# Gathering two instead of five pairs of round one's expert results ahead of round two's last down product

## The reference, cut to what matters

```python
top_scores, top_idx = jax.lax.top_k(sigmoid(xf @ gate_w.T), 2)       # 64 experts, 2 per token
buf = zeros((64, CAP, d)).at[flat_e, pos].set(x_pairs)               # tokens sorted by expert
h = silu(einsum('ecd,edh->ech', buf, w1)) * einsum('ecd,edh->ech', buf, w3)
y = einsum('ech,ehd->ecd', h, w2)
routed = (y[flat_e, pos].reshape(-1, 2, d) * top_scores[..., None]).sum(1)
shared = silu(xf @ sw1) * (xf @ sw3) @ sw2
out = h_res + shared + routed
```

## Time and profile before

| | us |
|---|---|
| median of three timed runs | 250.8 |
| lowest and highest of them | 248.49 and 253.65 |
| span of the profiled execution, first to last instruction | 258.9 |

### The profile page before, as it was taken

How to read it: one execution, slowest core, us unless ns; L and a number is a source line. 1 busy time by engine, 2 the same in 40 slices (tenths; PEclk the granted TensorE clock), 3 DMA queues, 4 the chain that set the end, 5 groups by cost and what they waited for, 6 DMA issues and landing times.

```text
span 258.9 us, 6074 instructions
## 1 busy us (share of the span) xinstructions
PE 187.3 (72%) x2479; PEld 154.5 (60%) x2479; DVE 152.3 (59%) x366; ACT 82.7 (32%) x245; POOL 146.2 (56%) x117
## 2 busy tenths in 40 slices
PE   0067967388899796994992997589888799619810
PEld 0067856267789585892991884368667677218410
DVE  0034364956778789689579557697896173001291
ACT  2005100032343432412411342356887342023500
POOL 3336499079989599986877673101516414730270
PEclk9999999779999999797798699657999999967975
DMA  7999999999999999999999995980013292310332
GB/s 256 236 385 420 372 417 329 418 417 417 416 421 424 416 421 413 422 404 391 297 213 232 206 148 85 293 233 5 0 38 109 70 279 60 93 32 21 103 95 52
DMA packets 32981, 65.11 MB, mean 251 GB/s; under 512 B 2874, under 2 KB 25367, under 8 KB 32375
## 3 DMA queue, kind: packets, MB, share of 16 engines
q1 hardware_dynamic: 31416, 59.47, 69.7%
q10 hardware_dynamic: 576, 3.26, 3.0%
q0 software_dynamic: 960, 1.97, 2.8%
HBM read 56.96 MB, written 7.73 MB: 250 GB/s over the span
## 4 chain that ended last, share of the span: by engine, by line
PE 37%; DMA 16%; DVE 16%; SPq 8%; ACT 5%; another core or an unknown queue 5%; POOL 4%; issue 4%; POOLq 1%; DVEq 0%; ACTq 0%
DMA ring<-in_L_tok_weight_dram 15%; PE bank L840 12%; PE bank L1000 4%; SPq L360 4%; PE bank L1030 4%; DVE ring L1220 3%; DVE bank L1250 3%; POOL ring L464 2%; DVE prod L1241 2%; PE bank L1014 2%; SPq L366 2%; PE bank L974 2%; PE bank L883 1%; PE bank L903 1%
## 5 line engine op out<-in xcount | busy, mean ns | idle before, releaser
L464 POOL TENSOR_TENSOR ring<-ring,mask 128x896 f32<-128x896 f32 (+1 forms) x48 | 92.1, 1945 | 18.4 <-DMA ring<-in_L_tok_weight_dram 18.4
L840 PE MATMUL bank<-ring,xT 128*64 128x128 f32 x1248 | 85.4, 295 | 10.6 <-DVE ring L1220 6.6
L840 PEld LDWEIGHTS bank<-ring,xT 128*64 128x64 f32 x1248 | 77.1, 149 | 16.1 <-DVE ring L1220 8.1
L1220 DVE TENSOR_TENSOR ring<-ring,bank 128x1024 f32<-128x1024 f32 (+1 forms) x45 | 45.7, 1048 | 34.7 <-DMA ring<-in_L_tok_weight_dram 34.6
L453 POOL TENSOR_TENSOR rstd<-mv,half 128x1 f32<-128x1 f32 (+1 forms) x24 | 14.3, 603 | 38.3 <-DVE mv L1228 22.8
L531 POOL DMA_INDIRECT ring<-expert_outputs,slot_index x16 | 16.1, 1007 | 26.6 <-DMA expert_outputs<-ring 22.3
L1000 PE MATMUL bank<-w,ring 128*64 128x128 f32 (+1 forms) x256 | 17.0, 322 | 8.0 <-ACT ring L692 5.7
L1000 PEld LDWEIGHTS bank<-w,ring 128*64 128x64 f32 (+1 forms) x256 | 12.9, 146 | 11.4 <-ACT ring L692 6.5
L506 POOL TENSOR_TENSOR mask<-ring,mask 128x256 f32<-128x256 f32 x8 | 7.5, 938 | 17.6 <-ACT ring L701 14.4
L821 PE MATMUL bank<-cst,w 64*128 64x64 f32 x39 | 5.3, 328 | 16.0 <-DMA w<-in_x_dram 15.4
L484 POOL DMA_INDIRECT expert_inputs<-xf,slot_index x14 | 14.3, 1022 | 4.1 <-issue 3.3
(11 more groups left out here) (151 smaller groups left out, 301.8 us busy)
## 6 DMA issues: line engine op xcount, KB each, us to landing
ring<-in_L_tok_weight_dram SPq DMA_DIRECT2D x48, 832.0 KB, 12.6
expert_inputs<-w ACTq DMA_DIRECT2D x3, 1024.0 KB, 9.9
ring<-expert_inputs SPq DMA_DIRECT2D x6, 512.0 KB, 5.4
expert_outputs<-ring SPq DMA_DIRECT2D x12, 256.0 KB
mask<-in_L_tok_mask_dram SPq DMA_DIRECT2D x3, 832.0 KB, 16.1
w<-in_x_dram SPq DMA_DIRECT2D x1, 1250.0 KB, 13.5
w2p<-in_L_ffn_w_dram SPq DMA_DIRECT2D x1, 1024.0 KB
xT<-masks_dram SPq DMA_DIRECT2D x1, 1024.0 KB, 7.9
```

Source lines behind the costliest of these rows:

```text
L464: pool.tensor_tensor(unit(j, q, SPLIT(q // 2), UC), unit(j, q, SPLIT(q // 2), UC), mask[:, (m + SPLIT(q // 2)) * D:(m + UC) * D], ALU.mult ...
L840: last = pe.matmul(bank[0][64 * par:64 * par + 64, 0:D], xT[:, (UC * t + c) * B:(UC * t + c + 1) * B], unit(j, 2 * t + par, c, c + 1), sta ...
L1220: dve.tensor_tensor(both(j, t, a, b), both(j, t, a, b), m.rearrange("p (u f) -> p u f", u=1).to_broadcast([P, 2, (b - a) * D]), ALU.mult). ...
```

## The change

The number of pairs gathered early falls from five to two, and the wait that stands between the early and the late gathers of round one is now on the last down product rather than on the last copy.

```diff
-GATHERED_EARLY = NCH1
+GATHERED_EARLY = 2
...
             for j in range(GATHERED_EARLY):
                 gather(j)
-            pool.wait_ge(s_ys, GROUPS)
+            pool.wait_ge(s_m2, GROUPS)
             for j in range(GATHERED_EARLY, NCH1):
                 gather(j)
```

## The result

The changed kernel took 254.12 us (median of four runs, 253.15 to 254.67). The kernel before, timed beside it, took 252.23 (four runs, 248.49 to 255.14). The ratio, here and in the experiments, compares only runs within 1.5% of the fastest of the same kernel beside it, which leaves out the 253.65 and 255.14 us of the kernel before. It is 1.0181, 95% interval 1.0095 to 1.0266: slower, by between 1.0 and 2.7%. The forecast was 253.5 us, a loss of 2.7 us (1.1%), with the larger part of the chance (0.65) on a change of less than 2% either way. The measured 1.81% is some 4.5 us, nearer to the rival without a stall (4.9 to 5.5 us) than to the forecast.

What follows compares the result with a forecast made beforehand. Bound by the last down product, its result's store, then six gathers on POOL, with a stall in round two. Median 250.8, minus 2.2 of stall won back, plus 4.9 for moved gathers: 253.5 us, range 246.0 to 256.5.

Steps and rivals of the forecast that it cites:

- the rival without a stall: Timed runs have no stall, so only the moved transfers on POOL count: 4.9 to 5.5 us slower, chance 0.29.
- Profile against timed runs: Most of the stall is absent without recording; a median run has 2.6 us, of which the change takes 2.2.
- the stall: Round two, around group 9: PE and ACT held up while ten early gathers follow one another on POOL; 10.7 us.
- What it adds: POOL at the end: six gathers moved behind the last down product, 7.83 us less 2.95 under the store, add 4.88.
- The bound upwards: Slower first gather and two more waits between tenth and eleventh gathers could raise the added 4.9 us to 5.5.
- What the stall is worth: Round two in the trace: 9.0 us of delay plus 1.8 us of low clock on PE, together 10.7 us.
- The signs: Changed profile: ACT's wait before group 9's Silu falls from 8.8 to 1-2 us, span about 255, timed runs don't fall.
- The stall is the chip's own: Round two's stall is as long in timed runs, so the trace's -4.0 us holds: 246.8 us, chance 0.25.
- The stall moves to the tail: Twelve gathers in a row beside the shared expert hold up its addition, 6.1 us over: 252.9 us, chance 0.04.

Runs made afterwards that it cites:

- the first and the fourth experiment: First: the kernel before, unedited, timed and traced again, ratio 1.0022. Fourth: the kernel before without any gathers of round one, ratio 0.9993.

## Why the prediction was wrong

**What failed** is the step "Profile against timed runs". It put the 8.1 us between the profiled span and the median run down to the stall, concluded that a median run has 2.6 us of it, and let the change win back 2.2. The runs show nothing won back. The second trace of the kernel before belongs to a run of 248.03 us and has no stall. The kernel without any early gather has the same times and as wide a spread. And with time = span + 1.7 us, a run with the first profile's span would be 260.6 us, 5.5 above the slowest of all 68 timed runs of the kernel before that I have (244.56 to 255.14). Even the fastest of these with the stall's 10.7 us added would be at 255.3, so hardly any timed run can have had the whole of it.

The step also set a span beside device times. With the 1.7 us the profiled execution was 9.8 us above the median run, not 8.1. The same step would then have left 0.9 us of stall in a median run, 0.7 to win back and a forecast of 250.8 - 0.7 + 4.9 = 255.0. Without the term the sum is the 4.9 us of the rival "no stall in the timed runs", 250.8 + 4.9 = 255.7 against 254.12 measured. As a ratio that is 1.020, where the result and the changed kernel's second set of runs have 1.018 and 1.020.

**What it adds** held: 4.88 us predicted; 4.8 in both traces of the changed kernel (8.6 against 3.8 from the last down product to the first gather of round two), with the price and the free room each shown by an experiment. The bound upwards was not needed: the two waits between the tenth and the eleventh gather cost nothing (0.30 us of idle time, as between any two). The whole way from round two's first transposition to the last instruction says the same:

```profile
208.55 1.16 PE L978 MATMUL bank<-cst,ring 128*128 128x128 f32 x8 [1.52 <-DMA ring<-expert_inputs]
```

```profile
212.90 1.16 PE L978 MATMUL bank<-cst,ring 128*128 128x128 f32 x8 [0.35 <-DMA ring<-expert_inputs]
```

In the second trace of the kernel before it is 246.3 - 208.55 = 37.8 us, in the second of the changed kernel 255.5 - 212.90 = 42.6: 4.8 more. It is 37.8 with four pairs early, 38.2 without the ten gathers and 39.9 with three pairs early. The first trace of the changed kernel has 44.0; 1.6 us of it are lost at the start, where PE takes 7.8 us to group 8's transposition at a granted clock of 0.78, against 6.2 at 1.00 in the kernel before.

**What the stall is worth** was well measured as a property of one execution (10.7 predicted; 24.3 - 13.5 = 10.8 in the traces) and wrongly taken for a property of the kernel. That transfers in a row on POOL are its cause was read from two places of one trace, at ten gathers and at four scatters. Ten, eight and fifteen gathers in a row elsewhere show nothing of the kind, nor do the same four scatters. All seven of PE's gaps that the first trace puts down to "issue" lie beside these two groups of transfers, and none of the nine later traces has one anywhere. So the transfers may have had a part in it, but not they alone. What else held PE up in that execution I can't say. None of the nine later traces has it again, so it could not be taken apart, and its cause stays open.

**The signs** came as forecast and were read too far. ACT's wait fell to 1.51 us, the span fell (to 251.4 us, not 255), and the timed runs did not. That was to show that the stall belongs to the recorded execution. It shows that one execution had it; the nine later traces were recorded as well, so recording alone doesn't bring it. Nor does the fall show what four gathers in place of ten do, since ten do the same.

**Rivals.** "The stall is the chip's own" would have given 246.8 and falls with the first and the fourth experiment. "The stall moves to the tail" has nothing to move. "No stall" had a chance of 0.29 and should have been the forecast. Its best argument stood in the text, that the span without the stall, 248.2 us, is a timed run that exists. With the 1.7 us it is 249.9, within 1 us of the median that I put against it.

The Trainium skill's figure of 6.2 us between a profile's total and the reported time ("Runtime: NRT & Kernel Launch", section "The ~15µs preamble/postamble breakdown") pointed the wrong way here: the reported time of every run is 1.7 us above the span. What the page means by the profile's total need not be this span.

## What to carry to other kernels

One trace shows what an execution did, not what a kernel does: a stall without a named releaser, in an execution that is longer than every timed run, is to be confirmed in a second trace before a change is credited with removing it. Work on a queue that ends ahead of its deadline is free where it stands: find the idle time between its end and the wait behind it (4.4 us here), and count what is moved past that wait at its full issue interval, less what still lies under the transfer that was waited for. Leaving such work out altogether is the cheapest way to learn that there is nothing to win from moving it.

## What the runs showed of the hardware

The runs of each of these kernels spread over some 5 to 10 us (the changed kernel's first four over 1.5). In the nine later traces round two begins anywhere from 205.91 to 212.90 us, 7.0 apart, and what follows differs by the gathers as told above. So far as the traces show, most of the spread arises ahead of round two. Two of them, 5.4 us apart there, in windows over the first 21 us of round one (columns as in rows 5), first the changed kernel's second trace, then that with fifteen gathers, whose program is the same up to there:

```profile
170.00:191.00 21.00, 19.23 (x153) 15.54 (x155) 16.54 (x30) 11.56 (x35) 4.95 (x5) 0.60 0.20 60
```

```profile
169.00:190.00 21.00, 18.01 (x222) 14.12 (x224) 18.88 (x33) 15.84 (x45) 6.32 (x7) 0.93 0.20 60
```

PE is busy for about the same time in both, but does 153 matmuls in the one and 222 in the other. The granted clock is a mean over the window, as a share of the full 2.4 GHz: 0.60, not far from the lower level of 1.2 GHz, and 0.93. A round-one up product, 16 matmuls, shows the two levels:

```profile
188.16 1.97 PE L1000 MATMUL bank<-w,ring 128*64 128x128 f32 x16
```

```profile
182.72 1.09 PE L1007 MATMUL bank<-w,ring 128*64 128x128 f32 x16
```

From the first transposition of round one to the first of round two it is 42.7 us (170.19 to 212.90) and 38.4 (169.11 to 207.48). PE's work ahead of these windows was much alike, 8.24 us busy in 12 and 7.23 in 11 us, at a granted clock of 0.71 and 0.67. So the same work is granted a different clock from execution to execution, and 4.3 of the 5.4 us are seen there. For an effect of 1 or 2% four runs of this kernel are few: here they left anything from 1.0 to 2.7% open.
